# Two parts for the second half of T's products, the exponential ahead of the last high piece, and the flip one slot further back

## The chip, the cores and the metric

The kernel runs on one core of a Trainium2 chip. The metric is the device time of one execution in microseconds (us); smaller is better. TensorE (PE) multiplies, VectorE (DVE), ScalarE (ACT) and GpSimd (POOL) do the elementwise work, and SyncE (SP) issues nearly all DMAs.

## What is computed

x is 16 images of 192 channels by 48 x 48 pixels (N = 2304 tokens). It is group-normalised, and an attention over channels (8 heads of 24) is added to it.

```python
qkv = xt @ w_qkv                      # xt: normalised x, (b, n, c)
q = q / max(sqrt(sum(q * q, over n)), EPS)
k = k / max(sqrt(sum(k * k, over n)), EPS)
k = k * temperature
attn = softmax(einsum('bhpn,bhnq->bhpq', k, q))      # (24 x 24) per head
out = einsum('bhnp,bhpq->bhnq', v, attn)
out = out @ w_out + b_out
return x + out
```

## The kernel before

**What it does per pair.** Nothing of the size of q, k or v is made. Two images go through together as a pair, and there are eight pairs. For each pair the kernel forms the Gram matrix G of the normalised channels, then T = G w (`t_mm`, tile `tq`), from it the scores and the squared norms (`scores`, `squares`), the softmax on 96 x 96 blocks, and a folded weight M = w_v attn w_out. The output is M times the normalised x, added to x. Float32 precision comes from splitting values into a high and a low float16 part: `h_sb` and `l_sb` are the parts of the normalised x, `wh`/`wl` those of the weights, `mh`/`ml` those of M.

**How it is staged.** `step(p)` runs for p = -1 to 7, on every engine with its own table of small steps. Phase A has 18 slots (`for j in range(SLOTS)`): in slot j PE multiplies the tokens `tok` of slot j of pair p+1 into G (`gram`), and transposes the tokens of slot j+3 (`transposes`, lines 1065 to 1068) into one of four PSUM banks, from which ACT copies them to `tok` (line 612). Between the slots stand the last small steps of pair p: `flip` (four 96 x 96 transposes of the scaled scores `qk_s`), `v` (`attn_values`, `s_ps<-wvh,ax`), and `m` (`folded_weights`). Phase B has 18 output blocks (`result`): PE multiplies pair p's block with M into a PSUM bank and DVE adds it to `x_sb` (line 937). Between the blocks stand the first small steps of pair p+1: `gram`, `w0` (T from G's upper rows), `w1` (T from the rest, through `z16`), `scores`, `squares`.

**What sets the order.** Each engine's tables give it: `PE_A`, `ACT_A`, `VEC_A` by slot of phase A, `PE_B`, `VEC_B` by block of phase B ("in 7" is inside block 7), `ACT_B` and `POOL_B` as plain lists that run without reference to blocks. The usual tables hold for phase B of p = 0 to 5 and phase A of p = 1 to 6; p = -1, phase A of p = 0, phase B of p = 6, and p = 7 have tables of their own (`FIRST_`, `SECOND_`, `LAST_`). Engines wait for each other by semaphores alone, and an engine runs its queue in the order in which it is written.

**The steps that matter here.**

- *x0 to x8, h0 to h8* (ACT, lines 565 and 574): the nine chunks (128 x 768) of the normalised x of a later pair, in float32 (`xn`, a ring of three) and as the high float16 part. POOL's line 502 subtracts them to the low part. x of chunk c waits for POOL's low part of chunk c-3. h6 to h8 stand in slots 2, 4 and 6 of phase A, the others in phase B. x0 waits for the group norm's scale `rb`.
- *w1*: `gram_weights(q, True)` does `shared_rows` (four matmuls into `s_ps`, the rows that both images share) and `whole_rows` (four matmuls into `g_ps`). ACT's t2 reads the shared rows, t0 and t1 the whole ones (line 664). DVE's steps of the same names (lines 914 and 923) follow, then `lo` (line 930), which `squares` on PE waits for.
- *norms*: DVE's line 836 takes the squared norms; POOL's line 519 raises them to the power -1/2 (`r8`).
- *spread* (DVE line 842) waits for `r8` and makes `qk_s`; PE's `flip` waits for it (line 1191); *soft_in* (lines 852 to 857) waits for the flip; ACT's *exp* (line 618) waits for it; *soft_out* (lines 865 to 874) waits for exp; PE's `v` waits for that. "bn" are pieces of the group norm's statistics of a later pair (line 798), put in between.

Of the kernel before, what the change touches and what calls it, by code (L numbers as in the profile page):

```python
# [65 lines left out]

PE_A = {0: ["flip"], 8: ["v"], 11: ["m"]}
PE_B = {0: ["gram"], 1: ["sums"], "in 4": ["w0"], "in 7": ["w1"], 11: ["scores"], 13: ["squares"]}  # L70
ACT_A = {2: ["h6"], 4: ["h7"], 6: ["h8"], 7: ["exp"], 11: ["v"], 14: ["m"]}
ACT_B = ["x0", "x1", "x2", "h0", "h1", "t2", "t0", "t1", "h2", "x3", "x4", "p", "h3", "h4", "x5", "h5", "x6", "x7", "x8"]
POOL_B = ["power", 0, 1, 2, 3, 4, 5, "norms", 6, 7, 8]
VEC_A = {0: ["soft_in"], 3: ["soft_out"], 7: ["v"], 11: ["m0"], 13: ["m1"], 17: ["stats"]}
VEC_B = {0: ["gram"], 1: ["var"], 3: ["z"], 5: ["t2"], 7: ["t0", "t1"], 10: ["lo"], 13: ["norms"], 17: ["bn", "bn", "spread", "bn", "bn"]}


FIRST_PE_A = {17: ["sums"]}
# [24 lines left out]
LAST_VEC_B = {0: ["gram"], 1: ["z"], 2: ["y2", "y0", "y1", "l2", "lo"], 3: ["l0", "l1", "norms"], 6: ["spread"], 9: ["soft_in"], 11: ["soft_out"], 14: ["v"]}  # L103
SUMS_AT = next(n for n, what in PE_B.items() if "sums" in what)


def preact_attention(nc, x, w_qkv, temperature, w_out, b_out, ident, ident16, groups, headmask, out):
# [30 lines left out]
    with ExitStack() as ctx:  # L138
        def sb(name, shape, dt=F32):
            return ctx.enter_context(nc.sbuf_tensor(name, shape, dt))  # L140
# [11 lines left out]
        w0 = sb("w0", [P, 3 * C])  # L152
        w1 = sb("w1", [P, 3 * C])
# [858 lines left out]
        def _(pe):  # L1012
# [89 lines left out]
                    wide(g_ps[:, b, :], e16[:, b, :], False)  # L1102
                    corner(g_ps[:, b, :], e16[:, b, :], True).then_inc(gfull, 1)

            def gram_weights(q, ready):


                z = z16
                if q == 0:

                    if not ready:
                        pe.wait_ge(high_ok, 1)
                    pe.wait_ge(low_ok, 4 if ready else 2)
                if ready:

                    pe.wait_ge(z_ok, q + 1)
                def whole_rows():
                    for b in (0, 1):
                        dst = g_ps[:, b, 0:2 * C]
                        hi, lo = (q16[:, b, i, 0:P] for i in (0, 1))  # L1120
                        if not ready:

                            pe.wait_ge(gl_ok, 2 * q + b + 1)
                            mm(dst, hi, wh0[:, :], True)
                            mm(dst, hi, wl0[:, :], False)
                            mm(dst, lo, wh0[:, :], False)
                        else:
                            mm(dst, z[:, b, 0:P], wh1[:, :], False)
                            mm(dst, z[:, b, 0:P], wl1[:, :], False, True).then_inc(t_mm, 1)

                def shared_rows():
                    if not ready:

                        need(pe, ml_ok, 2 * q)
                    for k in (range(3, 5) if ready else range(3)):
                        for b in (0, 1):
                            dst = s_ps[C1 * b:C1 * b + C1, 0, 0:2 * C]
                            hi, lo = (q16[:, b, i, P:C] for i in (0, 1))
                            lhs, rhs = ((hi, wh0), (hi, wl0), (lo, wh0), (z[:, b, P:C], wh1), (z[:, b, P:C], wl1))[k]
                            last = mm(dst, lhs, rhs[:, :], k == 0, k == 4)  # L1140
                    if ready:
                        last.then_inc(t_mm, 1)

                if ready:
                    shared_rows()
                    whole_rows()
                    return
                whole_rows()
                shared_rows()
                if q == 0:  # L1150

                    pe.wait_ge(gstep, GVAR + 1)
                pe.wait_ge(zb_ok, 2 * q + 2)
                for b in (0, 1):
                    for half in (0, 1):
                        last = nc.tensor.transpose(z_ps[:, b, P * half:P * half + P],
                                                   zb[:, b, 2 * half:2 * half + 2, :].rearrange("p i c -> p (i c)"), id16[:, 0:P])
                last.then_inc(z_mm, 1)
# [70 lines left out]
            def result(q, par, n, sums, between):  # L1229
                (t, c), w = OUTS[n], BW  # L1230
                h, l = (a[:, par, :, :] for a in (h_sb, l_sb))

                def bank_free(n):
                    if n >= RING:

                        pe.wait_ge(out_ok, (q + 1) * NO + n - RING + 1)
                    elif isinstance(q, int) and q == PAIRS - 1:

                        pe.wait_ge(out_ok, q * NO + NO - RING + (n + SLOTS) % RING + 1)

                def lower_weights(n, start):
                    at = OUTS[n][1]
                    return mm(block_ps(n), ml1[:, 1, :], h[:, 1, at:at + w], start, not start)

                def two_halves(start):
                    dst = block_ps(n)
                    for b in (0, 1):
                        mm(dst[C1 * b:C1 * b + C1, :], mh1[:, b, P - P * b:C - P * b], hl[:, b, c:c + w], start)
                    for k, (m, a) in enumerate(((mh0, h), (mh0, l), (ml0, h))):
                        for b in (0, 1):  # L1250
                            last = mm(dst[C1 * b:C1 * b + C1, :], m[:, b, P:C], a[:, 2 * b, c:c + w], False,
                                      k == 2 and not start)
                    return last

                def high_rows(n):
                    t, c = OUTS[n]
                    x = slice(c, c + w)
                    mm(block_ps(n), mh0[:, t // 2, 0:P], h[:, t, x], True)
                    mm(block_ps(n), mh0[:, t // 2, 0:P], l[:, t, x], False)

                in_front = RING if q == PAIRS - 1 else 0
                if n == 0:
                    if in_front:

                        pe.wait_ge(mh_ok, 3 * q + 1)
                    for k in range(in_front):
                        bank_free(k)
                        high_rows(k)

                    pe.wait_ge(mh_ok, 3 * q + 3)  # L1270
                    pe.wait_ge(ml_ok, 2 * q + 2)
                if n != 5 and n >= in_front:
                    bank_free(n)
                if n % (NO // GROUPS) == 0:

                    pe.wait_ge(hl_in[n // (NO // GROUPS)], (q + 1) * 64)
                if t != 1:
                    b, dst, x = t // 2, block_ps(n), slice(c, c + w)
                    if n >= in_front:
                        high_rows(n)  # L1280
                    mm(dst, mh1[:, b, C1 * b:C1 * b + P], hl[:, b, x], False)
                    mm(dst, ml0[:, b, 0:P], h[:, t, x], False)
                    mm(dst, ml1[:, t, :], h[:, 1, x], False, True).then_inc(out_mm, 1)
                elif n in (4, 16):
                    if sums:

                        pe.wait_ge(gstep, (q + 2) * GVAR + 1)
                    lower_weights(n, True)
                    if n == 4:
                        bank_free(n + 1)  # L1290
                        lower_weights(n + 1, True)
                    between()
                    two_halves(False).then_inc(out_mm, 1)
                elif n == 5:
                    two_halves(False).then_inc(out_mm, 1)
                elif n == 17:
                    two_halves(True)
                    lower_weights(n, False).then_inc(out_mm, 1)
                else:
                    two_halves(True)  # L1300
                    if n == 7:
                        between()
                        for k in (6, 7):
                            lower_weights(k, False).then_inc(out_mm, 1)

            small_steps = {"gram": finish_gram, "w0": lambda q: gram_weights(q, False),
                           "w1": lambda q: gram_weights(q, True), "scores": scores, "squares": squares, "flip": flip,
                           "v": attn_values, "m": folded_weights}

            def step(p, par=None, half=None):  # L1310
# [12 lines left out]
                for j in range(SLOTS):  # L1323
                    if more:
                        gram(p + 1, j)
                        if j + AHEAD < SLOTS:
                            transposes(p + 1, 1 - par, j + AHEAD)
                    for what in hooks(p, FIRST_PE_A, PE_A, LAST_PE_A, PAIRS - 1, SECOND_PE_A).get(j, ()):
                        if what == "sums":
# [65 lines left out]
```

## Time and profile before

| | |
|---|---|
| Median of 3 runs | 361.16 us (360.43 to 361.5) |
| The profiled execution | 360.94 us, of which the span that the trace covers is 359.1 us |
| Busy: PE, DVE, ACT, POOL | 87%, 79%, 68%, 41% of the span |
| Granted PE clock over the span | 0.988 of full |
| One usual pair | 39.8 us (in the chain that ended last, the last slots' gram starts at 194.22 and at 233.98 us) |

Read it so: times are us from the span's start. PE rows carry a modelled end, so the distance from one start to the next is the better measure of what a matmul takes. A row's bracket is the idle time of the engine ahead of it, and who ended it.

### The profile page before, as it was taken

Reading aid. Unit: us, or ns where it says so; the run is one execution under the profiler, and the core shown is the slowest. Engines: PE = TensorE matmul, PEld = TensorE weight load, DVE = VectorE, ACT = ScalarE, POOL = GpSimd, SP = SyncE. Lnnn points to the kernel's source line nnn. Section 1 sums busy time; section 2 is a strip of 40 time slices with the busy share of each in tenths; the row PEclk is TensorE's granted clock in tenths of the full one; section 3 lists DMA queues with packets and bytes.
Section 4 is the critical chain, followed back from the end, with each engine's and each line's share of the span. In section 5 each row is a group of like instructions: output and inputs, shape, how many; then the busy total and the mean of one; then the engine's idle time right before and its main releaser. Section 6 shows DMA issues by size and latency. Waiting matters only on the chain.

```text
span 359.1 us, 9368 instructions
## 1 busy us (share of the span) xinstructions
PE 313.7 (87%) x3692; PEld 221.4 (62%) x3692; DVE 284.6 (79%) x705; ACT 244.5 (68%) x447; POOL 146.0 (41%) x129
## 2 busy tenths in 40 slices
PE   0049868999989999999999999999999999999895
PEld 0037646765677657766577557766677557856552
DVE  4999895995989598986989598977989596269874
ACT  1088589759976698659976798659876799640300
POOL 0059679205750287215750387015840486002000
PEclk9999988999999999999999999999999999999999
DMA  7999920015993299715993499627991465016776
GB/s 218 352 300 252 248 70 3 3 42 159 297 330 102 99 282 289 257 55 148 310 330 87 134 299 306 189 89 192 297 317 34 161 188 181 3 47 175 259 219 226
DMA packets 30828, 67.75 MB, mean 189 GB/s; under 512 B 5504, under 2 KB 12096, under 8 KB 30784
## 3 DMA queue, kind: packets, MB, share of 16 engines
q1 hardware_dynamic: 30544, 66.56, 59.9%
q10 hardware_dynamic: 240, 0.59, 0.7%
q8 instruction: 29, 0.48, 0.6%
q14 instruction: 15, 0.12, 0.1%
HBM read 29.38 MB, written 28.31 MB: 161 GB/s over the span
## 4 chain that ended last, share of the span: by engine, by line
PE 54%; DVE 23%; ACT 8%; issue 8%; DMA 2%; SPq 2%; POOL 1%; ACTq 0%; DVEq 0%; POOLq 0%
PE u_ps L1014 23%; PE g_ps L1014 14%; PE s_ps L1014 9%; DVE x_sb L937 6%; ACT tok L612 3%; ACT h_sb L574 3%; PE u_ps L1065 2%; DVE pw L930 2%; DMA wo<-in_L_conv_w_out_dram 2%; DVE bnst L798 2%; PE u_ps L1066 2%; ACT xn L565 1%; DVE tq L914 1%; DVE g_ps L923 1%; PE u_ps L1068 1%
## 5 line engine op out<-in xcount | busy, mean ns | idle before, releaser
L502 POOL TENSOR_TENSOR l_sb<-xn,h_sb 128x768 f16<-128x768 f32 x63 | 102.9, 1654 | 49.6 <-ACT h_sb L574 49.4
L937 DVE SCALAR_TENSOR_TENSOR x_sb<-u_ps,bias,x_sb 128x384 f32<-128x384 f32 x144 | 84.0, 611 | 16.6 <-PE u_ps L1014 16.0
L1014 PE MATMUL g_ps<-tok 128*128 128x64 f16 (+1 forms) x864 | 86.5, 240 | 2.4 <-ACT tok L612 2.3
L612 ACT COPY tok<-u_ps 128x384 f32<-128x384 f32 x144 | 65.5, 481 | 18.6 <-PE u_ps L1068 17.1
L1014 PEld LDWEIGHTS g_ps<-tok 128*128 128x128 f16 x864 | 57.6, 99 | 24.9 <-ACT tok L612 3.9
L798 DVE BATCH_NORM_STATS2 bnst<-x_sb 128x6 f32<-128x384 f32 x144 | 70.3, 543 | 3.3 <-DMA x_sb<-in_x_dram 3.3
L1014 PE MATMUL u_ps<-h_sb,ml 128*128 128x384 f16 (+1 forms) x336 | 72.7, 326 | 0.0
L565 ACT ACTIVATE xn<-x_sb,rb 128x768 f32<-128x768 f32 x60 | 59.4, 1023 | 16.4 <-POOL rb L514 14.0
L574 ACT ACTIVATE h_sb<-x_sb,rb 128x768 f16<-128x768 f32 x63 | 63.5, 1030 | 0.4 <-POOL rb L514 0.4
L1065 PE MATMUL u_ps<-id,h_sb 128*128 128x128 f16 x288 | 49.3, 225 | 6.1 <-DVE l_sb L778 5.3
L508 POOL TENSOR_TENSOR grs<-gvar,minus_half 128x3 f32<-128x3 f32 x8 | 7.1, 885 | 104.1 <-DVE gvar L831 104.1
L1066 PE MATMUL u_ps<-id,l_sb 128*128 128x128 f16 x288 | 49.4, 225 | 0.0
L1014 PE MATMUL u_ps<-hl,mh 128*128 128x384 f16 (+1 forms) x192 | 47.5, 330 | 0.1
L1014 PE MATMUL u_ps<-h_sb,mh 128*128 128x384 f16 (+1 forms) x192 | 47.2, 327 | 0.0
L1014 PE MATMUL u_ps<-l_sb,mh 128*128 128x384 f16 (+1 forms) x192 | 47.1, 326 | 0.0
L1014 PEld LDWEIGHTS u_ps<-h_sb,ml 128*128 128x128 f16 (+1 forms) x336 | 28.7, 101 | 20.1 <-issue 3.0
L1067 PE MATMUL u_ps<-id,h_sb 128*128 128x128 f16 x144 | 32.4, 225 | 0.0
L1068 PE MATMUL u_ps<-id,l_sb 128*128 128x128 f16 x144 | 32.3, 224 | 0.0
L1065 PEld LDWEIGHTS u_ps<-id,h_sb 128*128 128x128 f16 x288 | 27.5, 101 | 6.6 <-ACT h_sb L581 5.4
L1066 PEld LDWEIGHTS u_ps<-id,l_sb 128*128 128x128 f16 x288 | 29.0, 101 | 0.4
L1014 PEld LDWEIGHTS u_ps<-hl,mh 128*128 128x128 f16 (+1 forms) x192 | 14.7, 103 | 11.9 <-issue 3.1
L519 POOL TENSOR_TENSOR r<-n,minus_half 96x8 f32<-96x8 f32 x8 | 13.6, 1702 | 20.5 <-DVE n L836 20.5
(149 smaller groups left out, 527.2 us busy)
## 6 DMA issues: line engine op xcount, KB each, us to landing
x_sb<-in_x_dram SPq DMA_DIRECT2D x48, 384.0 KB, 5.5
out_dram<-x_sb SPq DMA_DIRECT2D x48, 384.0 KB, 3.0
out_dram<-x_sb SPq DMA_DIRECT2D x48, 192.0 KB, 3.2
x_sb<-in_x_dram SPq DMA_DIRECT2D x45, 192.0 KB, 4.5
hl<-h_sb SPq DMA_DIRECT2D x48, 96.0 KB, 3.1
hl<-l_sb SPq DMA_DIRECT2D x48, 96.0 KB, 3.3
x_sb<-in_x_dram ACTq DMA_DIRECT2D x3, 192.0 KB, 4.6
w<-in_L_conv_w_qkv_dram SPq DMA_DIRECT2D x1, 288.0 KB, 8.0
```

The lines of the kernel that those rows point to most:

```text
L502: nc.gpsimd.tensor_tensor(l_sb[:, par, t, cols], xn[:, c % XN_RING, :], h_sb[:, par, t, cols], ALU.subtract).then_inc(l_ok, 1)
L519: nc.gpsimd.tensor_tensor(r8[:, :], n8[:, :], minus_half[0:HC, :].to_broadcast([HC, 8]), ALU.pow).then_inc(r8_ok, 1)
L565: nc.scalar.activation(xn[:, c % XN_RING, :], xcol(q, t, g * GW, GW), ACT.Identity, bias=rb[:, par, 1, t:t + 1], scale=rb[:, par, 0, t:t + ...
L574: nc.scalar.activation(h_sb[:, par, t, g * GW:g * GW + GW], xcol(q, t, g * GW, GW), ACT.Identity, bias=rb[:, par, 1, t:t + 1], scale=rb[:, ...
L612: nc.scalar.copy(tok[:, j % TOK_RING, :, :].rearrange("p b n -> p (b n)").bitcast(F32), slot_words(j)).then_inc(tok_a, 1)
L798: ins = V.bn_stats(bnst[:, t, 6 * part:6 * part + 6], xcol(q, t, part * BW, BW))
L937: V.scalar_tensor_tensor(out=xs, in0=block_ps(n), scalar=bias[:, t:t + 1], in1=xs, op0=ALU.add, op1=ALU.add).then_inc(out_ok, 1)
L1014: return nc.tensor.matmul(dst, lhs, rhs, start=start, stop=stop, skip_group_check=True)
L1065: nc.tensor.transpose(bank[:, b, 0:P], h_sb[:, par, 2 * b, px], id16[:, 0:P])
L1066: nc.tensor.transpose(bank[:, b, 256:384], l_sb[:, par, 2 * b, px], id16[:, 0:P])
L1067: nc.tensor.transpose(bank[:, :, P:P + C1], h_sb[:, par, 1, px], id16[:, 0:P])
L1068: nc.tensor.transpose(bank[:, :, P + C1:P + 2 * C1], l_sb[:, par, 1, px], id16[:, 0:P]).then_inc(tr_mm, 1)
```

## The change

Five tables change, and `gram_weights` takes an argument. On PE, `w1` becomes two steps: the shared rows run behind block 5, the whole rows stay inside block 7. ACT takes t2 ahead of h1, and the exponential ahead of h8 (slot 6) where it stood behind the copy of slot 7. PE's flip stands behind slot 1, not slot 0. DVE's spread has one statistics piece ahead of it and three behind it, not two and two. No instruction is added or removed, and no wait's value changes. `between()` is a call that runs the table's steps "in n".

```diff
-PE_A = {0: ["flip"], 8: ["v"], 11: ["m"]}
-PE_B = {0: ["gram"], 1: ["sums"], "in 4": ["w0"], "in 7": ["w1"], 11: ["scores"], 13: ["squares"]}
-ACT_A = {2: ["h6"], 4: ["h7"], 6: ["h8"], 7: ["exp"], 11: ["v"], 14: ["m"]}
-ACT_B = ["x0", "x1", "x2", "h0", "h1", "t2", "t0", "t1", "h2", "x3", "x4", "p", "h3", "h4", "x5", "h5", "x6", "x7", "x8"]
+PE_A = {1: ["flip"], 8: ["v"], 11: ["m"]}
+PE_B = {0: ["gram"], 1: ["sums"], "in 4": ["w0"], "in 5": ["w1 shared"], "in 7": ["w1 whole"], 11: ["scores"], 13: ["squares"]}
+ACT_A = {2: ["h6"], 4: ["h7"], 6: ["exp", "h8"], 11: ["v"], 14: ["m"]}
+ACT_B = ["x0", "x1", "x2", "h0", "t2", "h1", "t0", "t1", "h2", "x3", "x4", "p", "h3", "h4", "x5", "h5", "x6", "x7", "x8"]
...
-VEC_B = {0: ["gram"], 1: ["var"], 3: ["z"], 5: ["t2"], 7: ["t0", "t1"], 10: ["lo"], 13: ["norms"], 17: ["bn", "bn", "spread", "bn", "bn"]}
+VEC_B = {0: ["gram"], 1: ["var"], 3: ["z"], 5: ["t2"], 7: ["t0", "t1"], 10: ["lo"], 13: ["norms"], 17: ["bn", "spread", "bn", "bn", "bn"]}
...
-            def gram_weights(q, ready):
+            def gram_weights(q, ready, rows=""):
...
                 if ready:
-                    shared_rows()
-                    whole_rows()
+                    if rows != "whole":
+                        shared_rows()
+                    if rows != "shared":
+                        whole_rows()
                     return
...
                 elif n == 5:
                     two_halves(False).then_inc(out_mm, 1)
+                    between()
```

The first place is ACT in phase A, slots 3 to 10 of a usual pair. `tok<-u_ps` is the copy of a slot's tokens, `h_sb<-x_sb,rb` are h7 and h8, `s_ps<-s_ps` is the exponential. Before:

```order
L574 ACTIVATE h_sb<-x_sb,rb 128x768
L612 COPY tok<-u_ps 128x384 x2
L574 ACTIVATE h_sb<-x_sb,rb 128x768
L612 COPY tok<-u_ps 128x384
L618 ACTIVATE s_ps<-s_ps 96x96
L612 COPY tok<-u_ps 128x384 x4
```

After:

```order
L574 ACTIVATE h_sb<-x_sb,rb 128x768
L612 COPY tok<-u_ps 128x384 x2
L618 ACTIVATE s_ps<-s_ps 96x96
L574 ACTIVATE h_sb<-x_sb,rb 128x768
L612 COPY tok<-u_ps 128x384 x5
```

The exponential has moved ahead of h8 and of the copy of slot 7.

The second place is DVE at the end of phase B and the start of phase A: the last result blocks, the statistics pieces (`bnst<-x_sb`), the spread (`qk_s<-s_ps,r`) and the first step of soft_in. Before:

```order
L937 SCALAR_TENSOR_TENSOR x_sb<-u_ps,bias,x_sb 128x384 x4
L798 BN_STATS bnst<-x_sb 128x6 x2
L842 TENSOR_TENSOR qk_s<-s_ps,r 96x384
L798 BN_STATS bnst<-x_sb 128x6 x2
L852 TENSOR_TENSOR lg<-s_ps,mask 96x384
```

After:

```order
L937 SCALAR_TENSOR_TENSOR x_sb<-u_ps,bias,x_sb 128x384 x4
L798 BN_STATS bnst<-x_sb 128x6
L842 TENSOR_TENSOR qk_s<-s_ps,r 96x384
L798 BN_STATS bnst<-x_sb 128x6 x3
L852 TENSOR_TENSOR lg<-s_ps,mask 96x384
```

One of the four pieces has gone from ahead of the spread to behind it.

The third place is PE in phase B, from the end of block 5 (the last of the `two_halves` of blocks 4 and 5) to the whole rows. `s_ps<-wh,z` and `s_ps<-wl,z` are the shared rows, `g_ps<-wh,z` the first of the whole rows. Before:

```order
L1014 MATMUL u_ps<-h_sb,ml 64x384 x2
L1014 MATMUL u_ps<-hl,mh 64x384 x2
L1014 MATMUL u_ps<-h_sb,mh 64x384 x2
L1014 MATMUL u_ps<-l_sb,mh 64x384 x2
L1014 MATMUL u_ps<-h_sb,ml 64x384 x2
L1014 MATMUL u_ps<-hl,mh 64x384 x2
L1014 MATMUL u_ps<-h_sb,mh 64x384 x2
L1014 MATMUL u_ps<-l_sb,mh 64x384 x2
L1014 MATMUL u_ps<-h_sb,ml 64x384 x2
L1014 MATMUL s_ps<-wh,z 64x384 x2
L1014 MATMUL s_ps<-wl,z 64x384 x2
L1014 MATMUL g_ps<-wh,z 128x384
```

After:

```order
L1014 MATMUL u_ps<-h_sb,ml 64x384 x2
L1014 MATMUL s_ps<-wh,z 64x384 x2
L1014 MATMUL s_ps<-wl,z 64x384 x2
L1014 MATMUL u_ps<-hl,mh 64x384 x2
L1014 MATMUL u_ps<-h_sb,mh 64x384 x2
L1014 MATMUL u_ps<-l_sb,mh 64x384 x2
L1014 MATMUL u_ps<-h_sb,ml 64x384 x2
L1014 MATMUL u_ps<-hl,mh 64x384 x2
L1014 MATMUL u_ps<-h_sb,mh 64x384 x2
L1014 MATMUL u_ps<-l_sb,mh 64x384 x2
L1014 MATMUL u_ps<-h_sb,ml 64x384 x2
L1014 MATMUL g_ps<-wh,z 128x384
```

The four matmuls of the shared rows have moved ahead of the sixteen of blocks 6 and 7.

## Rows read from the trace of the kernel before

**Rows 1.** The page: share of the chain that ended last, by engine.

```profile
PE 54%; DVE 23%; ACT 8%; issue 8%; DMA 2%; SPq 2%; POOL 1%; ACTq 0%; DVEq 0%; POOLq 0%
```

**Rows 2.** Waits of PE, 90 to 300 us: total us, times, longest.

```profile
PE s_ps L1014 <- DVE ax L874: 4.0, 5, 0.8
PE s_ps L1014 <- DVE pw L930: 3.9, 6, 0.6
PE s_ps L1191 <- DVE qk_s L842: 1.2, 5, 0.2
```

**Rows 3.** Timeline, PE, one pair: start, duration, engine, line, operation, tiles, idle before.

```profile
202.75 0.33 PE L1014 MATMUL u_ps<-h_sb,ml 128*64 128x384 f16 x2
...
204.22 0.33 PE L1014 MATMUL s_ps<-wh,z 128*64 128x384 f16 x2
...
212.53 0.75 PE L1014 MATMUL s_ps<-side,pw 128*128 128x2 f16 x24 [0.64 <-DVE pw L930]
...
217.69 0.62 PE L1014 MATMUL g_ps<-tok 128*128 128x384 f16 x6
...
218.88 0.53 PE L1191 MATMUL s_ps<-id,qk_s 96*96 96x96 f32 x4 [0.24 <-DVE qk_s L842]
...
220.03 0.60 PE L1014 MATMUL g_ps<-tok 128*128 128x384 f16 x6
...
224.69 0.60 PE L1014 MATMUL g_ps<-tok 128*128 128x384 f16 x6
...
226.42 0.28 PE L1014 MATMUL s_ps<-wvh,ax 96*96 96x192 f16 x1 [0.79 <-DVE ax L874]
```

**Rows 4.** Timeline, DVE, the same pair.

```profile
205.80 0.36 DVE L914 TENSOR_TENSOR tq<-s_ps,tq 128x192 f16<-128x192 f32 x1 [2.05 <-ACT tq L664]
...
217.36 1.01 DVE L798 BATCH_NORM_STATS2 bnst<-x_sb 128x6 f32<-128x384 f32 x2
218.28 0.54 DVE L842 TENSOR_TENSOR qk_s<-s_ps,r 96x384 f32<-96x384 f32 x1
...
219.67 0.54 DVE L852 TENSOR_TENSOR lg<-s_ps,mask 96x384 f32<-96x384 f32 x1
...
221.69 0.26 DVE L857 TENSOR_TENSOR s_ps<-s_ps,mx 96x96 f32<-96x96 f32 x1
221.86 1.00 DVE L798 BATCH_NORM_STATS2 bnst<-x_sb 128x6 f32<-128x384 f32 x2
223.83 0.26 DVE L865 TENSOR_REDUCE sm<-s_ps 96x4 f32<-96x96 f32 x1 [0.97 <-ACT s_ps L618]
...
225.81 0.55 DVE L874 TENSOR_TENSOR ax<-s_ps,ax 96x384 f16<-96x384 f32 x1
```

**Rows 5.** Timeline, ACT, the same pair.

```profile
203.63 1.93 ACT L574 ACTIVATE h_sb<-x_sb,rb 128x768 f16<-128x768 f32 x2
...
216.07 1.03 ACT L565 ACTIVATE xn<-x_sb,rb 128x768 f32<-128x768 f32 x1 [0.39 <-POOL l_sb L502]
217.16 1.24 ACT L612 COPY tok<-u_ps 128x384 f32<-128x384 f32 x3
...
222.26 1.04 ACT L574 ACTIVATE h_sb<-x_sb,rb 128x768 f16<-128x768 f32 x1
223.19 0.48 ACT L612 COPY tok<-u_ps 128x384 f32<-128x384 f32 x1
223.55 0.25 ACT L618 ACTIVATE s_ps<-s_ps 96x96 f32<-96x96 f32 x1
```

**Rows 6.** Timeline, POOL, the same pair.

```profile
211.17 4.87 POOL L502 TENSOR_TENSOR l_sb<-xn,h_sb 128x768 f16<-128x768 f32 x3 [1.59 <-ACT h_sb L574]
215.98 1.67 POOL L519 TENSOR_TENSOR r<-n,minus_half 96x8 f32<-96x8 f32 x1
```

**Rows 7.** Timeline, PE, the pair of p = 6.

```profile
298.01 0.50 PE L1191 MATMUL s_ps<-id,qk_s 96*96 96x96 f32 x4
...
305.52 0.28 PE L1014 MATMUL s_ps<-wvh,ax 96*96 96x192 f16 x1 [0.79 <-DVE ax L874]
```

More of the change, by code:

```diff
@@ L1306, in _ @@
             small_steps = {"gram": finish_gram, "w0": lambda q: gram_weights(q, False),
-                           "w1": lambda q: gram_weights(q, True), "scores": scores, "squares": squares, "flip": flip,
+                           "w1": lambda q: gram_weights(q, True), "w1 shared": lambda q: gram_weights(q, True, "shared"),
+                           "w1 whole": lambda q: gram_weights(q, True, "whole"), "scores": scores, "squares": squares, "flip": flip,
                            "v": attn_values, "m": folded_weights}
```

## The prediction

> **What bounds the kernel now.** I read the page's chain of work first. It runs through PE for 54% and DVE for 23% of the span [rows 1]: PE is nearly always busy, and where it isn't, it waits for DVE. The table of PE's waits says where. In the stretch of the usual pairs only three waits are left, once per pair: for `ax` ahead of `v` (0.8 us), for `pw` ahead of `squares` (0.64 us), for `qk_s` ahead of the flip (0.24 us) [rows 2, 3]. The change aims at all three. Then I read one pair (194 to 234 us) engine by engine, since removing a wait pays only if nothing else is late there. The pairs repeat to 0.1 us, so I work out one and multiply.
>
> Sizes from starts on PE: gram of slot 2 starts at 220.03 and that of slot 8 at 224.69 us, so a slot takes 4.66/6 = 0.777 us. Gram 0 starts at 217.69, so slot 0 would end at 218.47; the flip starts at 218.88, 0.41 us later (the profile's 0.24 us leaves out modelled tails). Gram 1 must have started at 220.03 - 0.78 = 219.25, so the flip itself costs PE 0.37 us. Slot 8 ends at 224.69 + 0.78 = 225.47 and `v` starts at 226.42: 0.95 us lost [rows 3].
>
> **The change part by part.**
>
> **1. Shared rows earlier.** The four matmuls start at 204.22 us now; behind block 5 they start at 202.75 + 0.16 = 202.9 us (eight rows of 0.16 us lie between) [rows 3]. That is 1.3 us sooner, at no cost in instructions. ACT runs h0 and h1 from 203.63 us, 1.93 us for the two with an overlap of 0.10, so h0 hands over at 204.55 us and t2 can run there, 0.92 us sooner [rows 5]. DVE has been idle for 2.05 us ahead of its t2 [rows 4], so it and all that follows on DVE move up by 0.8 to 0.9 us, results 6 and 7, t0, t1 and `lo` with it. PE's wait of 0.64 us for `pw` goes. ACT's own queue gets no shorter: h1 slips 0.2 us, t0 starts where it did.
>
> What is late next? Gram 0 needs ACT's copy of slot 0. That copy starts at 217.16, 0.48 us long for one, and ends at 217.64 us; gram 0 starts at 217.69 [rows 3, 5]. So gram 0 already waits for ACT. Ahead of the copy stands x8, which starts at 216.07 because it waits for POOL's low part of chunk 5, the third of three from 211.17 us (ending at 216.04) [rows 5, 6]; POOL in turn waited for ACT's h3. This chain of ACT and POOL holds nothing that the change speeds up. x8 hands over at about 216.07 + 0.93 = 217.00 us (0.93 is the distance from h8 to the copy behind it, 222.26 to 223.19 [rows 5]), so the copy can come 0.16 us sooner, no more. **Of the 0.64 us only 0.16 us arrive at gram 0.** This is where I part from the plain sum of the waits. Bounds: 0 and 0.64 us per pair.
>
> **2. Flip behind slot 1.** PE does gram 1 and its transposes where it waited. By starts: gram 0 at 217.53, gram 1 at 218.31, flip at 219.08, gram 2 at 219.08 + 0.37 = 219.45 us against 220.03: 0.58 us sooner, 0.16 of them from part 1. The flip itself is 0.20 us later than now.
>
> **3. Spread one piece earlier, three pieces behind it.** DVE's last result comes 0.64 us sooner, but the spread needs POOL's power, which stands behind the three low parts: 215.98 + 1.67 = 217.65 us [rows 6]. So the spread starts at 217.70 us, not at 218.28 [rows 4], and DVE idles ahead of it. The pieces are 0.46 us apart (217.36 to 218.28 for two); three behind the spread end the run at 217.70 + 0.46 + 3 x 0.46 = 219.54. The flip ends at 219.08 + 0.53 = 219.61. Soft_in starts at 219.65 us against 219.67 [rows 4]: the flip's later place is paid for, and nothing is gained in the softmax yet.
>
> **4. Exponential ahead of h8.** Soft_in ends at 221.69 + 0.26 = 221.95 now [rows 4], the exponential runs only at 223.55, behind h8 and a copy [rows 5]. Ahead of them it runs at 221.95 and ends at 222.20 us. DVE's two pieces end at 222.86, and it then idles 0.97 us until 223.83 [rows 4]. That idle time goes in full, and no more, since the pieces now end last. `ax` ends at 225.81 + 0.55 = 226.36 now, 0.99 us sooner then: 225.37, and `v` starts at 225.43 us against 226.42. **0.99 us per pair.**
>
> Is PE there by then? Its gram 8 would start at 219.45 + 6 x 0.777 = 224.11, and it would arrive at 224.89 us. But ACT's queue is in the way: with the exponential at 221.95, h8 starts at 222.20, the copy of slot 7 at 223.13 and ends at 223.61 us, while gram 7 would be due at 223.34. PE loses 0.3 us and arrives at 225.2 us, still 0.2 us ahead of `ax`. The low part of chunk 8 starts no later than now, since h8 starts at 222.20 against 222.26 us. The Trainium skill (TensorE: Matmul & The Clock Gate, Architectural detail) says that ACT works strictly first in, first out. By that rule the exponential holds h8 and the copy of slot 7 while it waits; it speaks against this edit, and the trace agrees in that h8 and the copy run in the order of the table. If ACT's order could be relaxed, the 0.3 us would be nothing and the sum would not change, because `ax` is later.
>
> From `v` on, phase A hangs on `v` and moves as one.
>
> **The pair of p = 6.** Here DVE has no statistics pieces. The flip follows slot 0 without a wait, at 298.01 us, and `v` starts at 305.52 [rows 7]. The flip comes 0.78 - 0.16 = 0.62 us later: 298.63. Soft_in then starts at its end, 299.17, and ends 2.28 us later (221.95 - 219.67) at 301.45; the exponential ends at 301.71, and `ax` 2.53 us behind (223.83 to 226.36) at 304.28. PE arrives at 305.52 - 0.95 - 0.16 + 0.25 = 304.65 us, the last term for the same copy of slot 7. 0.9 us.
>
> **The sum.** Five pairs of 0.99 and one of 0.9 are 5.85 us. Against the profiled execution's 360.94 us this gives 355.1; that execution lies 0.2 us under the median of 361.16, and from the median it is **355.3 us**, 1.6% faster.
>
> **The rivals.**
>
> *Part 1 arrives in full.* If the chain through x8 has more room than it seems, gram 0 comes 0.64 us sooner. Yet `ax` still hangs on POOL's power (217.65), so soft_in starts at 219.54 at best, 0.13 us sooner than now: 6 x 1.12 = 6.7 us, 354.4 us. For it: nothing in the rows; against it: x8's wait for POOL. Chance 0.08.
>
> *ACT's order costs PE more.* If the copies of slots 5 to 7 come later than worked out, gram 7 and gram 8 set `v`, not `ax`. With 0.3 us more, `v` comes at 225.7 us, a gain of 0.7 us: 6 x 0.7 = 4.2, 357.0 us. For it: PE would be only 0.2 us ahead. Chance 0.14.
>
> *The gain is given back later in the pair* (the statistics, DMA, or the next group norm turn out to be due at fixed times): 361 us. The chain shows DMA with only 2%, at the start. Chance 0.04.
>
> *Slower.* Place: ACT's queue in slot 6. The exponential waits at its head for soft_in. If soft_in ended more than 1.2 us later than 221.95 us, gram 7 would start past 224.77, and `v` past its present 226.42 (three distances: h8 0.93, copy 0.48, slots 7 and 8 1.55). Each further us costs 6 us over the run: soft_in at 224.2 us gives 367 us. That needs the spread to be held, and POOL's power, which it waits for, hangs on ACT's h3 to h5. h3 would slip if t2 held ACT; but the shared rows end by 203.4 us and t2's turn comes at 204.55, 1.1 us of room. Chance 0.04.
>
> **How the numbers follow.** The forecast, gains of 5 to 6.4 us, has 0.70; part 1 in full 0.08; ACT's order 0.14; given back 0.04; slower 0.04. The range 354.3 to 357.1 us covers the first three. A measurement of this kernel tells 0.3%, 1.1 us, from no change: faster 0.92, same 0.04, slower 0.04.
>
> **What would show it.** In the trace after: DVE's idle time ahead of t2 falls from 2.05 to about 1.1 us; PE's wait for `pw` is gone, and a wait of some 0.5 us for `tok` stands ahead of gram 0 in its place; DVE waits for POOL ahead of the spread; no wait ahead of the flip; DVE's idle time for the exponential is gone; PE's wait for `ax` is 0.2 us where it was 0.95 by starts; a pair takes 38.8 us. If gram 0 comes 0.5 us or more sooner, part 1 was sized wrong. If PE's wait for `ax` is gone altogether, ACT's order was. The forecast is wrong if the exponential doesn't come by 222.3 us in its pair's clock.

## The result, and the profile after

The changed kernel takes 354.57 us (median of 4 runs) against 360.84 us before: ratio 0.982, 95% interval 0.980 to 0.985, so 6.3 us or 1.8% less. 355.3 us and 354.3 to 357.1 us had been forecast. The profiled execution took 353.76 us, its span 352.0.

The table of PE's waits in the stretch of the usual pairs, which answers to [rows 2]: total us, times, longest.

```profile
PE g_ps L1014 <- ACT tok L612: 3.8, 6, 0.6
```

All three old waits are gone. One has come: gram waits for ACT's copy of slot 0 in each pair, 0.6 us. PE's timeline of the pair that answers to [rows 3] shows where (start, duration, then as there):

```profile
198.76 0.33 PE L1014 MATMUL u_ps<-h_sb,ml 128*64 128x384 f16 x2
198.92 0.33 PE L1014 MATMUL s_ps<-wh,z 128*64 128x384 f16 x2
...
207.62 0.75 PE L1014 MATMUL s_ps<-side,pw 128*128 128x2 f16 x24
...
213.52 0.61 PE L1014 MATMUL g_ps<-tok 128*128 128x384 f16 x6 [0.64 <-ACT tok L612]
214.30 0.60 PE L1014 MATMUL g_ps<-tok 128*128 128x384 f16 x6
215.08 0.49 PE L1193 MATMUL s_ps<-id,qk_s 96*96 96x96 f32 x4
215.41 0.61 PE L1014 MATMUL g_ps<-tok 128*128 128x384 f16 x6
...
218.52 0.60 PE L1014 MATMUL g_ps<-tok 128*128 128x384 f16 x6
219.53 0.61 PE L1014 MATMUL g_ps<-tok 128*128 128x384 f16 x6
220.31 0.60 PE L1014 MATMUL g_ps<-tok 128*128 128x384 f16 x6
...
221.32 0.28 PE L1014 MATMUL s_ps<-wvh,ax 96*96 96x192 f16 x1
```

To compare clocks I add 3.98 us to the times of the changed trace: POOL's power, which stands behind the same three low parts in both, starts at 212.00 and at 215.98 us [rows 6], and the `v` of the pair ahead gives 3.99.

The shared rows follow block 5 at once and `squares` doesn't wait: it starts at 211.60 us in the clock of the kernel before, 0.93 us sooner than the 212.53 of [rows 3]. Gram 0 starts at 217.50, only 0.19 us sooner, and now has a bracket of 0.64 us itself. The flip has no bracket. Between gram 6 and gram 7 lie 1.01 us where a slot takes 0.78: gram 7 starts when ACT's copy of slot 7 is done.

DVE in the same pair, which answers to [rows 4]:

```profile
200.88 0.36 DVE L914 TENSOR_TENSOR tq<-s_ps,tq 128x192 f16<-128x192 f32 x1 [1.13 <-ACT tq L664]
...
212.44 0.55 DVE L798 BATCH_NORM_STATS2 bnst<-x_sb 128x6 f32<-128x384 f32 x1
213.69 0.55 DVE L842 TENSOR_TENSOR qk_s<-s_ps,r 96x384 f32<-96x384 f32 x1 [0.69 <-POOL r L519]
214.16 1.46 DVE L798 BATCH_NORM_STATS2 bnst<-x_sb 128x6 f32<-128x384 f32 x3
215.61 0.56 DVE L852 TENSOR_TENSOR lg<-s_ps,mask 96x384 f32<-96x384 f32 x1
...
217.65 0.26 DVE L857 TENSOR_TENSOR s_ps<-s_ps,mx 96x96 f32<-96x96 f32 x1
217.82 1.01 DVE L798 BATCH_NORM_STATS2 bnst<-x_sb 128x6 f32<-128x384 f32 x2
218.75 0.24 DVE L865 TENSOR_REDUCE sm<-s_ps 96x4 f32<-96x96 f32 x1
...
220.71 0.55 DVE L874 TENSOR_TENSOR ax<-s_ps,ax 96x384 f16<-96x384 f32 x1
```

The idle time ahead of t2 fell from 2.05 to 1.13 us, and that for the exponential is gone. A new one stands ahead of the spread, 0.69 us for POOL's power. `ax` ends at 221.26 and `v` starts at 221.32 us; PE would have been there at 221.09 (220.31 + 0.78), so `ax` still ends last. ACT and POOL, which answer to [rows 5] and [rows 6]:

```profile
212.07 1.03 ACT L565 ACTIVATE xn<-x_sb,rb 128x768 f32<-128x768 f32 x1 [0.39 <-POOL l_sb L502]
213.00 1.22 ACT L612 COPY tok<-u_ps 128x384 f32<-128x384 f32 x3
...
217.95 0.23 ACT L618 ACTIVATE s_ps<-s_ps 96x96 f32<-96x96 f32 x1 [0.30 <-DVE s_ps L857]
218.09 1.02 ACT L574 ACTIVATE h_sb<-x_sb,rb 128x768 f16<-128x768 f32 x1
219.01 1.21 ACT L612 COPY tok<-u_ps 128x384 f32<-128x384 f32 x3
```

```profile
207.17 4.87 POOL L502 TENSOR_TENSOR l_sb<-xn,h_sb 128x768 f16<-128x768 f32 x3 [1.58 <-ACT h_sb L574]
212.00 1.65 POOL L519 TENSOR_TENSOR r<-n,minus_half 96x8 f32<-96x8 f32 x1
```

x8 waits 0.39 us for POOL as before, and the exponential waits 0.30 us at the head of ACT's queue, with h8 and the copy of slot 7 behind it.

Where the time went in the profiled executions: `v` starts at 226.42 before and 221.32 after, 5.10 us. One pair, from `v` to `v`, took 39.77 us (186.65 to 226.42) and now takes 38.66 (182.66 to 221.32): **1.11 us per pair**. At p = 6, `v` moved from 305.52 to 298.38 us, 7.14 in all. Of these, 5.53 are the five pairs with statistics pieces (1.08 to 1.12 each) and 0.92 that of p = 6. The remaining 0.69 us were there before the first changed step: the flip of p = 0, which no edit touches, stands at 59.84 against 60.53 us. They belong to these two executions. 5.53 + 0.92 = 6.45 us are the change's, and the medians differ by 6.3.

### The profile page after: what moved, and what is told of

Its sections match the earlier page's. It is cut to its first block, busy times and chain, and to the rows that moved or that the text cites. A ratio compares the mean times of both kernels' runs of the same rounds, so it can differ in the third digit from the quotient of the medians.

```text
span 352.0 us, 9368 instructions
## 1 busy us (share of the span) xinstructions
PE 311.4 (88%) x3692; PEld 221.2 (63%) x3692; DVE 285.1 (81%) x705; ACT 243.9 (69%) x447; POOL 145.9 (41%) x129
## 4 chain that ended last, share of the span: by engine, by line
issue 35%; POOL 19%; PE 17%; DVE 15%; ACT 8%; SPq 2%; DMA 2%; ACTq 0%; POOLq 0%; DVEq 0%
POOL l_sb L502 14%; PE u_ps L1014 6%; PE g_ps L1014 5%; DVE bnst L798 4%; ACT h_sb L574 3%; PE s_ps L1014 3%; POOL r L519 2%; ACT xn L565 2%; DMA wo<-in_L_conv_w_out_dram 2%; POOL grs L508 2%; DVE s_ps L854 2%; ACT tok L612 1%; DVE lg L852 1%; DVE x_sb L937 1%; PE u_ps L1065 1%
## 5 line engine op out<-in xcount | busy, mean ns | idle before, releaser
L612 ACT COPY tok<-u_ps 128x384 f32<-128x384 f32 x144 | 64.6, 481 | 15.5 <-PE u_ps L1068 14.5
```

The costliest lines, as they stand in the source:

```text
L612: nc.scalar.copy(tok[:, j % TOK_RING, :, :].rearrange("p b n -> p (b n)").bitcast(F32), slot_words(j)).then_inc(tok_a, 1)
```

## The experiments

All ratios are to the kernel before on the same chip, with their 95% interval; a difference in us is the difference of the ratios times 361. "v to v" is the length of a usual pair in the trace (p = 6 is given by itself where it matters).

**1. The exponential alone** (`exp_only`, on the kernel before).

```diff
-ACT_A = {2: ["h6"], 4: ["h7"], 6: ["h8"], 7: ["exp"], 11: ["v"], 14: ["m"]}
+ACT_A = {2: ["h6"], 4: ["h7"], 6: ["exp", "h8"], 11: ["v"], 14: ["m"]}
```

> The kernel before with one edit alone, the exponential ahead of h8. Theory (v starts when the later of two is there, DVE's ax or PE itself): in the clock of the pair at 194 us of before, ACT is free after the copy of slot 6 at 222.26 us, the exponential ends at 222.5, DVE's pieces end last, ax is there at about 225.3, but PE's slot 8 ends at 225.47, so v starts at 225.5 against 226.42 us: 0.92 us in each of six pairs, 5.5 us, ratio to before 0.985. PE's waits for pw (0.64) and for qk_s (0.24) stay, the one for ax is under 0.1 us. Rival (each edit gives back its own wait and no more, and the shared rows carry a third of it): 0.5 us or less per pair, under 3 us, ratio above 0.992.

Measured: 355.36 us, 0.984 (0.982 to 0.986), 5.8 us less; v to v 38.79 us, 0.98 less. The table of PE's waits of this run:

```profile
PE s_ps L1014 <- DVE pw L930: 3.9, 6, 0.6
PE s_ps L1191 <- DVE qk_s L842: 1.2, 5, 0.2
```

Two of the three old waits are still there, and yet nine tenths of the change's whole gain. The wait for `ax` is gone from the table. PE and DVE at the end of one pair:

```profile
222.16 0.60 PE L1014 MATMUL g_ps<-tok 128*128 128x384 f16 x6
222.94 0.25 PE L1014 MATMUL s_ps<-wvh,ax 96*96 96x192 f16 x1
```

```profile
222.21 0.55 DVE L874 TENSOR_TENSOR ax<-s_ps,ax 96x384 f16<-96x384 f32 x1
```

`ax` ends at 222.76, and `v` starts at 222.94, one slot behind gram 8: PE now arrives last. The rival falls.

**2. The exponential back** (`exp_back`, on the changed kernel): the edit above in reverse.

> The changed kernel with the exponential back behind the copy of slot 7. Theory: since the copies of slots 4 to 6 come sooner than before, the exponential runs 0.37 us later than in the changed kernel in the five pairs with statistics pieces, and 0.9 us later at p = 6, where PE hides 0.3 of it. 5 x 0.37 + 0.6 = 2.5 us more than the changed kernel, 3.9 us less than before, ratio to before 0.989. Rival (the exponential's place is worth its whole wait of 0.95 us per pair, and waits add up): 5.7 us more than the changed kernel, ratio 0.998.

Measured: 357.17 us, 0.990 (0.988 to 0.992), 3.6 us less than before and 2.7 more than the changed kernel; v to v 39.02 us, 0.36 more than there (0.37 expected). So one edit is worth 5.8 us alone and 2.7 as the last of four. It does not have a price of its own.

**3. The shared rows alone** (`shared_only`, on the kernel before).

```diff
-PE_B = {0: ["gram"], 1: ["sums"], "in 4": ["w0"], "in 7": ["w1"], 11: ["scores"], 13: ["squares"]}
+PE_B = {0: ["gram"], 1: ["sums"], "in 4": ["w0"], "in 5": ["w1 shared"], "in 7": ["w1 whole"], 11: ["scores"], 13: ["squares"]}
-ACT_B = [..., "h0", "h1", "t2", "t0", ...]
+ACT_B = [..., "h0", "t2", "h1", "t0", ...]
```

> The kernel before with the shared rows behind block 5 and t2 ahead of h1, and nothing else. Theory: PE's wait for pw goes, gram 0 comes only 0.16 us sooner and waits for tok, but the flip no longer waits for DVE, since the spread now hangs on POOL's power (217.65 us) and not on DVE's last result. Soft_in starts at 219.1 against 219.67 us, v at 225.84 against 226.42: 0.58 us in five pairs, 0.16 at p = 6, 3.0 us, ratio 0.992. Rival 1 (ACT's copy of slot 0 swallows all but 0.16 us per pair): 1.0 us, ratio 0.997. Rival 2 (part 1 arrives in full): 0.64 x 6 = 3.8 us with gram 0 coming 0.64 us sooner.

Measured: 357.65 us, 0.991 (0.990 to 0.993), 3.1 us less; v to v 39.17 us, 0.60 less (0.58 expected). PE's, DVE's and ACT's timelines of one pair:

```profile
210.10 0.75 PE L1014 MATMUL s_ps<-side,pw 128*128 128x2 f16 x24
...
216.00 0.62 PE L1014 MATMUL g_ps<-tok 128*128 128x384 f16 x6 [0.64 <-ACT tok L612]
216.79 0.53 PE L1193 MATMUL s_ps<-id,qk_s 96*96 96x96 f32 x4
```

```profile
216.17 0.55 DVE L842 TENSOR_TENSOR qk_s<-s_ps,r 96x384 f32<-96x384 f32 x1 [0.23 <-POOL r L519]
```

```profile
221.45 0.25 ACT L618 ACTIVATE s_ps<-s_ps 96x96 f32<-96x96 f32 x1
```

Ahead of gram 0 stands a wait for `tok` here too, so gram 0 gained only 0.17 us (counted from POOL's power: 1.54 us behind it, where it was 1.71). The 0.6 us came by the other way: DVE's blocks end sooner, the spread with them (it now waits for POOL, not for DVE's own queue), and the flip behind slot 0 finds its input ready. From there it went by another path than expected. Soft_in ends 0.58 us sooner (counted in the same way), at 219.85 us, but the exponential starts 1.6 us after that, because it still stands behind h8 and the copy of slot 7. Gram 1, which starts behind the flip, comes sooner, and ACT's copies and the exponential with it; run 8 shows this link again. Both rivals fall: 1.0 us is too little, and gram 0 didn't gain 0.64.

**4. The shared rows back** (`shared_back`, on the changed kernel): the edits of 3 in reverse.

> The changed kernel with the shared rows back at block 7 and t2 behind h1. Theory: DVE's last result is 0.64 us later, the spread starts at 217.82 against 217.68 us and gram 0 at 217.69 against 217.51; soft_in starts 0.18 us later, and v with it. 6 x 0.18 = 1.1 us more than the changed kernel, ratio to before 0.985. PE waits 0.64 us for pw again. Rival (the wait for pw counts in full): 3.8 us more, ratio 0.993.

Measured: 356.11 us, 0.987 (0.985 to 0.989), 1.6 us more than the changed kernel. The direction holds against the rival's 3.8 us; the size is 0.5 us over what was expected. The undisturbed pairs of this trace take 38.84 us, 0.18 more than in the changed kernel, as worked out. But two pairs are longer (39.35 and 39.15, 0.8 us together, which would cover the 0.5), and in both DVE waits for a load of x:

```profile
107.61 1.02 DVE L798 BATCH_NORM_STATS2 bnst<-x_sb 128x6 f32<-128x384 f32 x2 [0.70 <-DMA x_sb<-in_x_dram]
...
224.45 1.02 DVE L798 BATCH_NORM_STATS2 bnst<-x_sb 128x6 f32<-128x384 f32 x2 [0.51 <-DMA x_sb<-in_x_dram]
```

**5 and 6. Flip back, and spread back** (`flip_back` and `spread_back`, each on the changed kernel).

```diff
-PE_A = {1: ["flip"], 8: ["v"], 11: ["m"]}
+PE_A = {0: ["flip"], 8: ["v"], 11: ["m"]}
```

```diff
-VEC_B = {..., 17: ["bn", "spread", "bn", "bn", "bn"]}
+VEC_B = {..., 17: ["bn", "bn", "spread", "bn", "bn"]}
```

> The changed kernel with the flip back behind slot 0. Theory (soft_in hangs on POOL's power and the three statistics pieces behind the spread): PE's flip doesn't wait even there, since the spread ends 0.06 us ahead of slot 0's end, and soft_in starts at most 0.05 us sooner because the three pieces end last. Within 0.5 us of the changed kernel, rather under it; ratio to before 0.982. Rival (the flip's old wait of 0.41 us comes back): 2.5 us more than the changed kernel, ratio 0.989.

> The changed kernel with two statistics pieces ahead of the spread and two behind it, as before. Theory: the second piece fits into the 0.69 us in which DVE waits for POOL's power, so the spread starts at the same time, and soft_in then waits for the flip (behind slot 1) instead of the third piece. Within 0.3 us of the changed kernel, ratio 0.982. Rival (the spread is set by DVE's pieces, and comes 0.46 us later): soft_in waits for that, 2.8 us more, ratio 0.990.

Measured: flip back 353.70 us, 0.981 (0.979 to 0.983), v to v 38.58; spread back 354.45 us, 0.982 (0.980 to 0.985), undisturbed v to v 38.66. The intervals of both contain the changed kernel's 0.982. Taken out alone, each of the two edits seems to be worth next to nothing. The traces say what holds soft_in in each case. With the flip back (DVE, `flip_back`) it follows the three pieces, the flip having ended at 214.72 us (214.19 + 0.53):

```profile
214.05 1.46 DVE L798 BATCH_NORM_STATS2 bnst<-x_sb 128x6 f32<-128x384 f32 x3
215.44 0.53 DVE L852 TENSOR_TENSOR lg<-s_ps,mask 96x384 f32<-96x384 f32 x1
```

With the spread back (DVE, `spread_back`) it waits for the flip:

```profile
216.41 0.56 DVE L852 TENSOR_TENSOR lg<-s_ps,mask 96x384 f32<-96x384 f32 x1 [0.45 <-PE s_ps L1193]
```

The 0.08 us per pair of `flip_back` are small but stand in all its pairs: in the changed kernel soft_in starts 1.92 us behind the spread, just behind the flip's end, and in `flip_back` 1.86, just behind the pieces.

**7. Both back** (`both_back`): the diffs of 5 and 6 together, so that of the change only the shared rows and the exponential are left.

> The changed kernel with the flip behind slot 0 and two pieces on either side of the spread, both as before; the shared rows and the exponential as changed. Theory: each of the two alone is held by the other, and together they let soft_in start at 215.1 against 215.61 us in the changed kernel's clock. ax comes 0.5 us sooner, PE's slot 8 ends at 220.85, and v starts at 220.87 against 221.32 us: 0.45 us in five pairs and 0.2 at p = 6, 2.4 us less than the changed kernel, 352.2 us, ratio to before 0.976. Rival (the flip's and the spread's new places carry a part of the gain): more than 355.5 us.

Measured: **351.85 us, 0.975** (0.973 to 0.978), 2.5 us less than the changed kernel; v to v 38.19 us, 0.47 less (0.45 expected). DVE's and PE's timelines of one pair:

```profile
212.90 0.56 DVE L842 TENSOR_TENSOR qk_s<-s_ps,r 96x384 f32<-96x384 f32 x1 [0.22 <-POOL r L519]
213.38 1.00 DVE L798 BATCH_NORM_STATS2 bnst<-x_sb 128x6 f32<-128x384 f32 x2
214.30 0.54 DVE L852 TENSOR_TENSOR lg<-s_ps,mask 96x384 f32<-96x384 f32 x1
```

```profile
212.73 0.61 PE L1014 MATMUL g_ps<-tok 128*128 128x384 f16 x6 [0.62 <-ACT tok L612]
213.51 0.54 PE L1193 MATMUL s_ps<-id,qk_s 96*96 96x96 f32 x4
213.88 0.61 PE L1014 MATMUL g_ps<-tok 128*128 128x384 f16 x6
...
220.10 0.25 PE L1014 MATMUL s_ps<-wvh,ax 96*96 96x192 f16 x1
```

From the spread to soft_in (`lg`) it is 1.40 us, where the changed kernel has 1.92. The flip stands behind slot 0 and has no bracket. The change had put the flip later and a third piece ahead of soft_in; either one holds soft_in, which is why undoing one alone did next to nothing. `v` gains 0.47 us and not 0.52, since PE now arrives last (219.32, the start of gram 8, + 0.78 = 220.10). So two of the four edits cost the changed kernel 2.5 us.

**8. Those two edits alone** (`places_only`): the diffs of 5 and 6 in the other direction, on the kernel before.

> The kernel before with the flip behind slot 1 and one statistics piece ahead of the spread, three behind it, and nothing else: the two edits that cost 2.7 us on top of the other two (both_back against the changed kernel). Theory (what an edit is worth depends on what ends last): here the exponential stands at the end of ACT's queue, which hangs on the copy of slot 4 and so on PE's gram 1. With the flip behind slot 1, gram 1 comes 0.78 us sooner and the copy of slot 4 0.6 us, so the exponential starts at 223.05 against 223.55 us, although soft_in is 0.1 us later. v 0.5 us sooner in five pairs; at p = 6, where the flip didn't wait, nearly as much: 2.5 to 3 us less than before, ratio 0.992. Rival (the two edits cost what they cost there): 2.7 us more than before, ratio 1.0075.

Measured: 357.99 us, 0.992 (0.990 to 0.993), 3.0 us **less** than before; v to v 39.21 us, 0.56 less (0.5 expected), but at p = 6 only 0.11 less, where nearly as much had been expected. The profiled execution took 360.14 us, 2.2 over the median: one of its pairs is 2.6 us longer than the others, and DVE waits in it for loads of x, once for 0.69 us and once for 2.00:

```profile
114.82 1.02 DVE L798 BATCH_NORM_STATS2 bnst<-x_sb 128x6 f32<-128x384 f32 x2 [2.00 <-DMA x_sb<-in_x_dram]
```

ACT's timeline of one pair, whose slot 0 lies 0.44 us later than that of [rows 5] (217.60 for its first copy, not 217.16):

```profile
217.60 1.24 ACT L612 COPY tok<-u_ps 128x384 f32<-128x384 f32 x3
...
219.65 0.87 ACT L612 COPY tok<-u_ps 128x384 f32<-128x384 f32 x2
...
223.45 0.24 ACT L618 ACTIVATE s_ps<-s_ps 96x96 f32<-96x96 f32 x1
```

The copies of slots 3 and 4 now run back to back, and the exponential starts 5.85 us behind the first copy, where it was 6.39 [rows 5]. In the kernel before, ACT waited for PE ahead of the copy of slot 4:

```profile
220.23 0.48 ACT L612 COPY tok<-u_ps 128x384 f32<-128x384 f32 x1 [0.54 <-PE u_ps L1068]
```

The same two edits that cost 2.5 us on top of the others gain 3.0 without them: where the exponential waits for its turn on ACT, an earlier gram 1 lets ACT run sooner; where it stands ahead of h8, only soft_in counts, and they delay that. The rows point to the flip's place for the gain; the two edits were not run one by one on the kernel before.

**9. x8 out of the way** (`x8_late`, on the changed kernel).

```diff
-ACT_A = {2: ["h6"], 4: ["h7"], ...}
-ACT_B = [..., "x6", "x7", "x8"]
+ACT_A = {2: ["h6"], 3: ["x8"], 4: ["h7"], ...}
+ACT_B = [..., "x6", "x7"]
```

> The changed kernel with x8 taken out of the end of phase B and put behind the copy of slot 3 in phase A. Theory: gram 0 no longer waits for the chain of POOL's low part 5 and x8 and starts 0.5 us sooner, and that brings next to nothing, because ax hangs on POOL's power: at most 0.06 us per pair, 0 to 0.5 us less than the changed kernel, ratio to before 0.981 to 0.983. Rival (gram 0's wait for tok is what bounds the pair): 0.5 us per pair, 3 us less, ratio 0.974.

Measured: 353.64 us, 0.980 (0.978 to 0.982). In its trace PE's gram 0 starts 0.79 us behind the start of POOL's power (212.75 and 213.54), where it was 1.52 (212.00 and 213.52). So x8 was what held it: 0.73 us sooner. And `v` starts 9.25 us behind the power, where it was 9.32. 0.07 us of 0.73 arrive. PE waits for the copies of slots 5 and 7 instead, and `ax` still ends last (221.94, `v` at 222.00):

```profile
218.19 0.61 PE L1014 MATMUL g_ps<-tok 128*128 128x384 f16 x6 [0.25 <-ACT tok L612]
...
220.21 0.61 PE L1014 MATMUL g_ps<-tok 128*128 128x384 f16 x6 [0.30 <-ACT tok L612]
```

```profile
221.39 0.55 DVE L874 TENSOR_TENSOR ax<-s_ps,ax 96x384 f16<-96x384 f32 x1
```

The median is 0.9 us under the changed kernel's, the ratio 0.0025 under, with intervals that overlap: not told apart from the 0 to 0.5 that were expected. The rival's 3 us are ruled out.

**10 and 11. Going on from `both_back`.** `power_early` adds x8 as in 9 and

```diff
-POOL_B = ["power", 0, 1, 2, 3, 4, 5, "norms", 6, 7, 8]
+POOL_B = ["power", 0, 1, 2, 3, 4, "norms", 5, 6, 7, 8]
```

and `act_spaced` adds to that

```diff
-ACT_A = {2: ["h6"], 3: ["x8"], 4: ["h7"], 6: ["exp", "h8"], 11: ["v"], 14: ["m"]}
+ACT_A = {2: ["h6"], 3: ["x8"], 5: ["h7"], 6: ["exp"], 8: ["h8"], 11: ["v"], 14: ["m"]}
-VEC_B = {..., 17: ["bn", "bn", "spread", "bn", "bn"]}
+VEC_B = {..., 17: ["bn", "spread", "bn", "bn", "bn"]}
```

> The run both_back with two more edits: POOL's power of the norms ahead of its low part 5, and x8 (which waits for that low part) behind ACT's copy of slot 3. In both_back v waits neither for ax (there 0.17 us ahead) nor for tok; what PE loses is 0.62 us ahead of gram 0. Theory: gram 0 comes 0.6 us sooner and the spread 0.3 us sooner, but x8, h6, h7 and h8 now all stand between the copies of slots 2 and 7, ACT has no idle time left there, and the copies of slots 5 and 7 hold gram 5 and 7. v comes 0.1 us sooner: 0 to 1 us less than both_back, ratio to before 0.973 to 0.976. Rival (gram 0's wait is all that is left): 0.6 us in each of six pairs, 3.6 us less, ratio 0.966.

> power_early with h7 behind the copy of slot 5, h8 behind that of slot 8, and one statistics piece ahead of the spread, three behind it. Theory: the copies of slots 4 to 8 now come in time, PE arrives at v 0.6 us sooner than in both_back, and ax, 0.35 us sooner, ends last: v 0.48 us sooner in each pair, 2.9 us less than both_back, ratio to before 0.967. h8 starts at 218.3 us in both_back's clock, its low part ends at 221.1, and slot 12's transposes need it at 221.5. Rival (that low part comes late, since POOL's or ACT's queue slips by over 0.4 us): PE waits there, and the gain is under 1 us, ratio 0.973 or more.

Measured: `power_early` 351.02 us, 0.973 (0.970 to 0.975), about 1 us under `both_back`, with intervals that overlap; v to v 38.08, 0.11 less (0.1 expected). One cause was missed: at slot 0 the flip waits 0.23 us for `qk_s` again, since PE is there sooner than DVE. `act_spaced` **350.38 us, 0.970** (0.968 to 0.972), the lowest of all, though its interval overlaps that of `power_early`: 10.8 us less than before, with v to v 37.81 us. Its one remaining wait of PE:

```profile
218.66 0.28 PE L1014 MATMUL s_ps<-wvh,ax 96*96 96x192 f16 x1 [0.17 <-DVE ax L874]
```

It is 1.5 us (medians) to 1.9 us (ratios) under `both_back`, not 2.9. The pair got 0.38 us shorter, not 0.48: `ax` does end last, but came 0.28 us sooner (counted from `squares`), not 0.35. That explains 0.6 us over six pairs of the missing 1.0 to 1.4. The two profiled executions differ by 2.15 us (351.89 and 349.74), which leaves nearly nothing else to explain there; the rest lies between one execution and the next and stays open. The order of work on four engines, without an instruction less, is thus worth 3.0%, and the change took 1.8 of it.

## Why the prediction was right, and where it wasn't

**What bounds the kernel, and part 1.** Right where it mattered. Times from here on are in the clock of the kernel before (3.98 us added), but for those from PE's rows given with their sum. Gram 0 starts at 217.50 (217.53 forecast). Run 9 shows that x8 holds it, which in the trace waits for POOL's low part 5, and that freeing it in that way is worth 0.07 us per pair. Mis-sized, without effect: PE and DVE's last result came 0.93 us sooner, not 0.64. The bracket of `squares` was not all that PE lost there, so the wait ahead of gram 0 is 0.64 us and not about 0.5. That it equals the old wait for `pw` to the hundredth is chance.

**Part 2.** The flip starts at 219.06 (219.08) without a wait. It cost PE 0.33 us between starts (215.08 to 215.41), not 0.37. In runs where it starts 0.05 to 0.07 us behind the spread's end it costs 0.36 to 0.37 (`flip_back`, `both_back`, `shared_only`), in `act_spaced`, where the spread ends 0.11 us ahead of it, 0.34; so the 0.04 seem to belong to starting just as the input comes, which no run shows by itself.

**Part 3.** The spread starts at 217.67 (217.70), soft_in at 219.59 (219.65). The reading that soft_in gains next to nothing was right: 0.08 us. The 0.06 beyond the forecast come from the flip, which started 0.02 us sooner and took 0.49 us in its row, not 0.53. What the step left out is the question whether the edits should be there: it found the flip's later place "paid for", compared with the kernel before. Compared with the shared rows and the exponential alone, run 7 shows that the flip's and the spread's new places cost 2.5 us. The total was still right, since I had asked of all four together what ends last.

**Part 4.** The exponential starts at 221.93 (221.95). Mis-sized: soft_out starts at 222.73, not 222.84, and `v` at 225.30, not 225.43. Of these 0.13 us, 0.06 come from soft_in, and the rest from taking the end of the row of the two pieces (222.86) as the time at which DVE is free; the next instruction starts 0.08 us ahead of such a row's end (217.82 + 1.01 against 218.75). That is 1.11 us per pair where 0.99 were forecast, 0.6 us over five pairs, and nearly all that lies between the forecast 5.85 us and the 6.45 of the profiled executions. Of the 0.7 us between 355.3 and 354.57, 0.3 are only that the forecast started from a median of 361.16 us, and the kernel before has 360.84 here.

**PE's arrival.** ACT's order costs PE 0.24 us at gram 7 (1.01 against 0.777), 0.3 had been forecast; PE is there at 221.09 (220.31 + 0.78), 0.23 us ahead of `v`. The rival by which ACT's order would set the pair did not come.

**p = 6.** 0.92 us, 0.9 forecast. Nothing was given back later: 298.38 us for `v` and the span's end both moved by 7.1.

**The rivals.** Part 1 in full gave 354.4 us, which is nearer to 354.57 than the forecast's 355.3, and its 1.12 us per pair match the 1.11. The time alone would speak for it; the trace does not. It had gram 0 come 0.64 us sooner, and gram 0 came 0.19 us sooner here and 0.17 in run 3; and run 9 shows that 0.73 us at gram 0 bring 0.07 at `v`. The 0.12 us beyond the forecast come from the flip and from DVE's row, as told under parts 3 and 4, and that they make up the same sum is chance. "Given back later" fails by p = 6, and "slower", soft_in more than 1.2 us late, was never near.

## What to carry to other kernels

When several steps of one chain are moved, an edit has no price of its own: the exponential was worth 5.8 us alone and 2.7 last, and the flip's and the spread's places gained 3.0 us without the others and cost 2.5 with them. So work out what ends last for each subset, and once the large edits are in, take each small one out again, in pairs too, since two edits can hide behind each other. A wait that turns up again at the next place (0.64 us at `squares`, then at gram 0) is the sign that another engine's queue bounds that stretch, though it may be worth little to free it (0.07 us here). And a time that fits a rival as well as the forecast decides nothing; the row in which the two differ does (gram 0's start here).

## What the runs showed of the hardware

A DVE or ACT row ends later than the engine is free for an instruction that doesn't need the result: on DVE the next one started 0.08 us ahead of the row's end (217.82 + 1.01 against 218.75), on ACT 0.10 us (h8, 218.09 + 1.02 against 219.01).

Loads of x come late now and then for the statistics pieces behind `v`. In the usual pairs of one trace each, there is no such wait in the kernel before, the changed kernel, `exp_only`, `shared_only`, `flip_back` and `act_spaced`; in the others they are 0.15 to 0.70 us, and 2.00 us once. The length of the pair does not order them: the 2.00 us stand in `places_only` at 39.2 us per pair, and `act_spaced`, the shortest at 37.8, has none. No run here tells what brings them.
